# A block of fp32 matmuls ahead of the first projection of a fused attention layer

## The chip, the cores and the metric

The kernel runs on the 8 cores of one Trainium2 chip, as two dies of four cores. Each core does the same program on its own two sequences; the cores don't talk to each other. The metric is the device time of one execution in microseconds (us), that of the slowest core. Within 0.2% two kernels can't be told apart here.

## The reference, cut to what matters

x is [16, 2048, 1024] in fp32; every weight is 1024 x 1024.

```python
xn = layernorm(x)                                  # no gain, no bias
q, k, v = xn @ Wq.T, xn @ Wk.T, xn @ Wv.T          # 16 heads of 64
a = sliding_window_attention(q, k, v, 128)         # causal, chunks of 128 see their own and the previous chunk
s = a @ Wo.T
lhs_scale = max|xn| / 127 (by row);  rhs_scale = max|rhs| / 127 (by column)
q_lhs, q_rhs = round(xn / lhs_scale), round(rhs / rhs_scale)
g = silu((q_lhs @ q_rhs) * lhs_scale * rhs_scale)
y = x + s * g
```

## The kernel before, in words

A core's 4096 rows are worked in 32 chunks of 128 rows. The program is five instruction streams, one for each engine, each written out in full: an engine runs its stream in order, and waits on semaphores where it needs another's result. For each chunk TensorE (PE) makes five products of 128 x 1024 by 1024 x 1024 in bf16, each as 16 matmuls of 512 columns: `PROJ` for q, v, k and ffn into the PSUM tile `p_proj`, and the output product into `p_av`. Between them stand two groups of 16 score matmuls of 128 columns (`SCORES`, into `p_sc`) and 32 of 65 columns for attention times v (`AVS`, into `p_sc` again). ScalarE (ACT) empties `p_proj`, takes the exponentials and quantizes the rows; VectorE (DVE) does the layer norm (`LN1`, `LN2`), the mask, the division by the row sums, the ffn scaling and the result. The queue of SyncE (SP) issues the loads of x, the transposing DMAs and the stores. In the loop of a stream, step i does the main part of chunk i beside the projections of chunk i + 1 and the layer norm of chunk i + 2 or i + 3.

Ahead of the loop there is a prologue. GpSimd (POOL) issues the loads of the four attention weights, SP and ACT issue those of `rhs` in eight blocks, and DVE quantizes each block as it lands (lines 309 to 319). PE first works after the eighth block: one transpose of the eight column scales (line 495), which DVE copies to `rsrow8` (line 323), and then eight matmuls in fp32 (line 508) that spread the scales over all partitions in `p_proj`. DVE copies that out to `scr` (line 325), does `LN2(0)`, whose last instruction (line 294) writes the normalized chunk 0, and then `LN1(1)`. SP transposes `q_rhs` (line 161), loads chunks 1 and 2 of x (line 166) and transposes the quantized and the normalized chunk 0 (lines 210 and 214). PE's loop begins with `PROJ(0, "q", ...)`, whose matmuls all have line 519 and which waits for the transpose of chunk 0, for the q weights and for DVE's copy out of `p_proj`:

```python
                    Wv(tensor, f"trxn{c % 2}", 16 * (c // 2 + 1))
                    if c == 0:
                        Wv(tensor, "lwq", 128)
                    ...
                        W(tensor, "v", ("rsbe", 0))
                        PROJ(c, "q", bfp, XNT[c % 2], wbf, 0 * 8192)
```

`ident` is the 128 x 128 identity in fp32. `scr[:, XS[0]:...]` holds chunk 0 of x in fp32, loaded on the semaphore `lx0`. `IMM` issues a list of matmuls back to back and raises the semaphore `t` with the last of them. `Wv` waits for a semaphore's value, `W` for a named event.

Of the kernel before, what the change touches and what calls it, by code (L numbers as in the profile page):

```python
# [20 lines left out]
XS = [0, 1024, 2048, 3072]  # L21
# [52 lines left out]
def build(nchunk=NCHUNK):  # L74
# [15 lines left out]
    with ExitStack() as es:  # L90
# [3 lines left out]
        scr = sb("scr", [128, SCR_COLS], F32)  # L94
# [7 lines left out]
        ident = sb("ident_s", [128, 128], F32)  # L102
# [4 lines left out]
        p_sc = es.enter_context(nc.psum_tensor("p_sc", [128, 2048], F32))  # L107
# [21 lines left out]
        def Wv(eng, sname, value):  # L129
            if CUR[0].emit:  # L130
                eng.wait_ge(SEMS[sname], value)
# [361 lines left out]
        def emit_tensor(tensor):  # L493
# [5 lines left out]
            def IMM(mms, sname, tag):  # L499
                if CUR[0].emit:  # L500
                    last = None
                    for f in mms:
                        r = f()
                        last = r if r is not None else last
                    last.then_inc(SEMS[sname], 1)
                CUR[0].inc(sname, 1, (tag[0], tag[1]))
# [2 lines left out]
                                            sel[:, t * 128:(t + 1) * 128], rsrow8[:],  # L509
                                            start=True, stop=True)) for t in range(8)],  # L510
                "t", ("rsb", 0))

            def PROJ(c, name, lhs_t, lhs_base, rhs_t, rhs_base, half1_wait=None):
                mms = []
                for kc in range(8):
                    for half in range(2):
                        if kc == 0 and half == 1 and half1_wait is not None:
                            mms.append(half1_wait)
                        mms.append(lambda kc=kc, half=half: tensor.matmul(  # L519
                            p_proj[:, half * 512:(half + 1) * 512],  # L520
                            lhs_t[:, lhs_base + kc * 128:lhs_base + kc * 128 + 128],
                            rhs_t[:, rhs_base + kc * 1024 + half * 512:
                                  rhs_base + kc * 1024 + half * 512 + 512],
                            start=(kc == 0), stop=(kc == 7)))
                IMM(mms, "t", (name, c))
# [37 lines left out]
            for i in range(-2, nchunk + 2):  # L563
# [42 lines left out]
                if 0 <= i < nchunk:  # L606
# [7 lines left out]
                    for kc in range(8):  # L614
# [3 lines left out]
                        for half in range(2):  # L618
# [5 lines left out]
                                start=(kc == 0), stop=(kc == 7)))  # L624
# [25 lines left out]
        emit_vector(fe)  # L650
        emit_scalar(fe)
        emit_tensor(fe)
        emit_gpsimd(fe)

# [17 lines left out]
        @block.tensor  # L672
        def _(tensor):
            emit_tensor(tensor)
# [46 lines left out]
```

How the kernel before makes its waits and increments, by code:

```python
        def W(eng, sname, tag):  # L125
            if CUR[0].emit:
                eng.wait_ge(SEMS[sname], CUR[0].tag[(sname, tag)])
# [1 line left out]
        def Wv(eng, sname, value):  # L129
            if CUR[0].emit:
                eng.wait_ge(SEMS[sname], value)
# [1 line left out]
        def I(instr, sname=None, tag=None, n=1):  # L133
            if CUR[0].emit:
                bi = instr()
                if sname is not None:
                    bi.then_inc(SEMS[sname], n)
            if sname is not None:
                CUR[0].inc(sname, n, tag)
# [2 lines left out]
        def emit_sync(sync):  # L142
# [73 lines left out]
                      f"trxn{c % 2}", ("trxn", c), 16)  # L216
                if 0 <= i < nchunk:
                    c = i
                    b, cc = divmod(c, 16)
                    W(sync, "v", ("comb", c))
                    I(lambda b=b, cc=cc, c=c: sync.dma_start(
                        y_h[b, cc * 128:(cc + 1) * 128, :],
                        scr[:, OUTS[c % 2]:OUTS[c % 2] + 1024]),
                      "st", ("store", c), 16)
            if CUR[0].emit:
                sync.wait_ge(SEMS["st"], 16 * nchunk)
# [2 lines left out]
            def SW(instr):  # L229
                I(instr, "v", None)
                if CUR[0].emit:
                    vector.wait_ge(SEMS["v"], CUR[0].count["v"])
# [170 lines left out]
            def SWS(instr, sname=None, tag=None):  # L403
                I(instr, sname or "a", tag)
                if CUR[0].emit:
                    scalar.wait_ge(SEMS[sname or "a"], CUR[0].count[sname or "a"])
```

## Time and profile before

| | |
|---|---|
| median of 9 runs | 849.19 us (847.94 to 850.1) |
| the profiled execution, its own time | 848.81 us |
| span of its slowest core, from the first to the last instruction | 847.2 us |
| spans of the 8 cores | 841.5 to 847.2 us |
| PE busy | 665.2 us, 79% of the span |
| DVE busy | 530.0 us, 63% |
| ACT busy | 420.2 us, 50% |

The profiled execution's own time is 1.6 us more than the span of its slowest core: what lies around the first and the last instruction. The views below show core 4, unless another is named. An idle time is written beside the work that ended it, with the event that released that work.

### The profile page before, as it was taken

Reading aid. Unit: us, or ns where it says so; the run is one execution under the profiler, and the core shown is the slowest. Engines: PE = TensorE matmul, PEld = TensorE weight load, DVE = VectorE, ACT = ScalarE, POOL = GpSimd, SP = SyncE. Lnnn points to the kernel's source line nnn. Section 1 sums busy time; section 2 is a strip of 40 time slices with the busy share of each in tenths; the row PEclk is TensorE's granted clock in tenths of the full one; section 3 lists DMA queues with packets and bytes.
Section 4 is the critical chain, followed back from the end, with each engine's and each line's share of the span. In section 5 each row is a group of like instructions: output and inputs, shape, how many; then the busy total and the mean of one; then the engine's idle time right before and its main releaser. Section 6 shows DMA issues by size and latency. Waiting matters only on the chain.

```text
span 847.2 us, 13584 instructions; the slowest of 8 cores (841.5 to 847.2 us)
## 1 busy us (share of the span) xinstructions
PE 665.2 (79%) x4561; PEld 344.9 (41%) x4625; DVE 530.0 (63%) x1083; ACT 420.2 (50%) x481; POOL 17.2 (2%) x36
## 2 busy tenths in 40 slices
PE   0001588898889898888889888899888889988884
PEld 0001244444444444444444444444444444444442
DVE  3644257666666667766766666666776666666633
ACT  0001355556555566655555655556665555565541
POOL 8000000000000000000000000000000000000000
PEclk9999999999999999999999999999999999999995
DMA  7999245554444454444554434554335555444431
GB/s 162 197 208 189 61 82 107 112 107 105 89 89 111 113 112 97 101 103 106 106 113 112 99 86 91 113 113 113 94 97 110 106 107 112 113 100 89 63 63 62
DMA packets 194066, 91.29 MB, mean 108 GB/s; under 512 B 180296, under 2 KB 180680, under 8 KB 194000
## 3 DMA queue, kind: packets, MB, share of 16 engines
q1 hardware_dynamic: 188816, 79.95, 43.6%
q0 software_dynamic: 4608, 8.39, 6.2%
q10 hardware_dynamic: 576, 2.10, 0.8%
q8 instruction: 38, 0.62, 0.3%
q14 instruction: 28, 0.23, 0.1%
HBM read 37.98 MB, written 16.78 MB: 65 GB/s over the span
## 4 chain that ended last, share of the span: by engine, by line
PE 41%; DVE 30%; issue 14%; DMA 8%; ACT 3%; SPq 2%; DVEq 1%; ACTq 0%
PE p_proj L519 26%; PE p_av L619 12%; DVE sm L257 4%; DVE sm L247 4%; DVE scr L395 4%; DVE scr L384 4%; DVE bfp L341 3%; DMA scr<-rhst 3%; DVE scr L253 3%; DMA bfp<-bfp 3%; DVE scr L375 2%; DMA scr<-x 2%; SPq L161 1%; PE p_sc L555 1%; PE p_sc L558 1%
## 5 line engine op out<-in xcount | busy, mean ns | idle before, releaser
L519 PE MATMUL p_proj<-wbf,bfp 128*128 128x512 bf16 x1473 | 336.8, 381 | 61.0 <-DVE scr L375 22.9
L519 PEld LDWEIGHTS p_proj<-wbf,bfp 128*128 128x128 bf16 x1536 | 144.4, 98 | 224.0 <-issue 71.0
L619 PE MATMUL p_av<-wbf,bfp 128*128 128x512 bf16 x511 | 117.7, 384 | 4.2 <-DMA bfp<-bfp 3.1
L489 ACT ACTIVATE scr<-scr 128x1024 f32<-128x1024 f32 x32 | 33.8, 1057 | 174.5 <-DVE scr L375 174.5
L519 PE MATMUL p_proj<-qrhs,bfp 128*128 128x512 bf16 x512 | 115.7, 379 | 1.1 <-ACT bfp L474 1.1
L371 DVE SCALAR_TENSOR_TENSOR scr<-p_proj,sm,scr 128x512 f32<-128x512 f32 x32 | 24.0, 751 | 124.0 <-PE p_proj L519 123.9
L619 PEld LDWEIGHTS p_av<-wbf,bfp 128*128 128x128 bf16 x512 | 49.7, 99 | 67.9 <-issue 12.2
L519 PEld LDWEIGHTS p_proj<-qrhs,bfp 128*128 128x128 bf16 x512 | 50.0, 98 | 61.8 <-issue 1.5
L341 DVE TENSOR_TENSOR bfp<-bfp,mstd_s 128x2048 bf16<-128x2048 bf16 x60 | 71.0, 1222 | 4.7 <-ACT bfp L437 4.7
L459 ACT ACTIVATE q32t<-scr,sm 128x1024 int32<-128x1024 f32 x32 | 37.2, 1161 | 67.0 <-DVE bfp L319 67.0
L555 PE MATMUL p_sc<-bfp 128*128 128x65 bf16 x512 | 40.0, 195 | 36.4 <-DVE bfp L341 19.7
L536 PE MATMUL p_sc<-bfp 128*128 128x128 bf16 x512 | 64.8, 220 | 3.8 <-ACT bfp L421 3.8
L541 PE MATMUL p_sc<-bfp 128*128 128x128 bf16 x512 | 64.8, 220 | 0.0
L421 ACT ACTIVATE bfp<-p_sc 128x2048 bf16<-128x2048 f32 x32 | 59.5, 1859 | 0.0
L427 ACT CAST bfp<-p_proj 128x1024 bf16<-128x1024 f32 x32 | 32.4, 1012 | 49.5 <-PE p_proj L519 49.5
L555 PEld LDWEIGHTS p_sc<-bfp 128*128 128x128 bf16 x512 | 34.2, 98 | 53.2 <-issue 53.0
L536 PEld LDWEIGHTS p_sc<-bfp 128*128 128x128 bf16 x512 | 50.4, 99 | 11.6 <-issue 4.2
L495 PE MATMUL p_av<-ident_s,sm 128*8 128x128 f32 x1 | 0.4, 371 | 69.4 <-DVE bfp L319 69.4
L541 PEld LDWEIGHTS p_sc<-bfp 128*128 128x128 bf16 x512 | 50.4, 99 | 7.3
L443 ACT CAST bfp<-p_proj 128x512 bf16<-128x512 f32 x32 | 18.8, 589 | 65.1 <-PE p_proj L519 65.1
L247 DVE TENSOR_REDUCE sm<-scr 128x1 f32<-128x1024 f32 x32 | 38.8, 1211 | 15.8 <-DMA scr<-x 15.8
L384 DVE TENSOR_TENSOR scr<-p_av,scr 128x1024 f32<-128x1024 f32 x32 | 38.9, 1214 | 7.4 <-PE p_av L619 7.4
(63 smaller groups left out, 736.6 us busy)
## 6 DMA issues: line engine op xcount, KB each, us to landing
scr<-x SPq DMA_DIRECT2D x32, 512.0 KB, 4.6
y<-scr SPq DMA_DIRECT2D x32, 512.0 KB, 2.9
bfp<-bfp SPq DMA_TRANSPOSE x192, 3.2
scr<-rhst ACTq DMA_DIRECT2D x4, 512.0 KB, 8.1
wbf<-wqt POOLq DMA_DIRECT2D x8, 256.0 KB, 16.1
scr<-rhst SPq DMA_DIRECT2D x4, 512.0 KB
wbf<-wkt POOLq DMA_DIRECT2D x8, 256.0 KB, 25.5
wbf<-wvt POOLq DMA_DIRECT2D x8, 256.0 KB, 38.8
```

Source lines behind the costliest of these rows:

```text
L247: SW(lambda c=c: vector.reduce_sum(sm[:, SUMC:SUMC + 1], scr[:, XS[c % 4]:XS[c % 4] + 1024], AX.X))
L257: SW(lambda c=c, am=am: vector.reduce_max(sm[:, am:am + 1], scr[:, CEN[c % 2]:CEN[c % 2] + 1024], AX.X, apply_absolute_value=True))
L341: I(lambda e=ebv, r=erv, m=mkv: vector.tensor_tensor(e, r, m, ALU.mult), "v", ("e0m" if g == 0 else "e1m", c))
L384: SW(lambda c=c: vector.tensor_tensor(scr[:, T1_:T1_ + 1024], p_av[:, 0:1024], scr[:, GS[c % 2]:GS[c % 2] + 1024], ALU.mult))
L395: I(lambda c=c: vector.scalar_tensor_tensor(scr[:, GS[c % 2]:GS[c % 2] + 1024], scr[:, GS[c % 2]:GS[c % 2] + 1024], 1.0, scr[:, GPRE:GPRE ...
L421: I(lambda: scalar.activation(bfp2[:, ERAW:ERAW + 2048], p_sc[:, 0:2048], AF.Exp, scale=0.125), "a", ("e0", c))
L459: SWS(lambda c=c: scalar.activation(q32[:], scr[:, CEN[c % 2]:CEN[c % 2] + 1024], AF.Copy, scale=sm[:, QRA[c % 2]:QRA[c % 2] + 1], bias=MA ...
L519: mms.append(lambda kc=kc, half=half: tensor.matmul(p_proj[:, half * 512:(half + 1) * 512], lhs_t[:, lhs_base + kc * 128:lhs_base + kc * 1 ...
L536: mms.append(lambda hh=hh, qcol=qcol, tcol=tcol: tensor.matmul(p_sc[:, hh * 256:hh * 256 + 128], bfp[:, ktp + tcol:ktp + tcol + 128], bfp[ ...
L541: mms.append(lambda hh=hh, qcol=qcol, tcol=tcol: tensor.matmul(p_sc[:, hh * 256 + 128:hh * 256 + 256], bfp[:, ktc + tcol:ktc + tcol + 128] ...
L555: mms.append(lambda h=h, e0=e0: tensor.matmul(p_sc[:, h * 128:h * 128 + 65], bfp2[:, e0:e0 + 128], bfp[:, vp_ + h * 65:vp_ + h * 65 + 65], ...
L619: mms.append(lambda kc=kc, half=half, c=c: tensor.matmul(p_av[:, half * 512:(half + 1) * 512], bfp2[:, AOT[c % 2] + kc * 128:AOT[c % 2] + ...
```

## The change

One block of PE's prologue is new, between the eight matmuls that spread the scales and the loop. PE waits until chunk 0 of x is in SBUF, and then multiplies 512 columns of it by the identity, in fp32, 48 times, into the four banks of `p_sc` in turn. Nothing reads these results, and no other engine's stream is changed; the event `("warm", 0)` is waited for by nobody. The first scores of chunk 0 overwrite `p_sc`.

```diff
                                             sel[:, t * 128:(t + 1) * 128], rsrow8[:],
                                             start=True, stop=True)) for t in range(8)],
                 "t", ("rsb", 0))
+            Wv(tensor, "lx0", 16)
+            IMM([(lambda r=r: tensor.matmul(p_sc[:, (r % 4) * 512:(r % 4) * 512 + 512],
+                                            ident[:], scr[:, XS[0]:XS[0] + 512],
+                                            start=True, stop=True))
+                 for r in range(48)], "t", ("warm", 0))
 
             def PROJ(c, name, lhs_t, lhs_base, rhs_t, rhs_base, half1_wait=None):
```

## Rows read from the trace of the kernel before

**Rows 1.** The page, busy time by engine, and the slices of PE.
```profile
PE 665.2 (79%) x4561; PEld 344.9 (41%) x4625; DVE 530.0 (63%) x1083; ACT 420.2 (50%) x481; POOL 17.2 (2%) x36
...
PE   0001588898889898888889888899888889988884
```
**Rows 2.** PE's waits: who it waited for, us in total, times, longest.
```profile
PE p_av L495 <- DVE bfp L319: 69.4, 1, 69.4
PE p_proj L519 <- DVE scr L375: 22.9, 27, 0.8
...
PE p_proj L519 <- DVE sm L260: 15.4, 1, 15.4
```
**Rows 3.** Timeline, core 4: start, us, engine, line, operation, count, idle time before.
```profile
70.27 3.75 PE L508 MATMUL p_proj<-rsrow,sel_s 8*128 8x128 f32 x16 [0.53 <-DVE rsrow L323]
...
78.94 0.75 DVE L294 TENSOR_SCALAR bfp<-scr,sm 128x1024 bf16<-128x1024 f32 x1
...
83.67 3.41 SPq L214 DMA_TRANSPOSE bfp<-bfp  x1
...
89.46 5.22 PE L519 MATMUL p_proj<-wbf,bfp 128*128 128x512 bf16 x16 [15.44 <-DVE sm L260]
...
94.77 1.01 ACT L427 CAST bfp<-p_proj 128x1024 bf16<-128x1024 f32 x1 [21.91 <-PE p_proj L519]
...
96.03 3.61 PE L519 MATMUL p_proj<-wbf,bfp 128*128 128x512 bf16 x16 [1.36 <-ACT bfp L427]
```
**Rows 4.** Line 508, core 4: durations min/median/max, first and last start.
```profile
L508 PEld LDWEIGHTS p_proj<-rsrow,sel_s x16: 284/328/328, 70.2 to 73.4; 8*128 8x128 f32 x16
L508 PE MATMUL p_proj<-rsrow,sel_s x16: 416/416/549, 70.3 to 73.6; 8*128 8x128 f32 x16
```
**Rows 5.** Timeline, core 4: two weight loads among the first projection's matmuls.
```profile
90.27 0.15 PEld L519 LDWEIGHTS p_proj<-wbf,bfp 128*128 128x128 bf16 x1 [0.28 <-issue]
90.70 0.15 PEld L519 LDWEIGHTS p_proj<-wbf,bfp 128*128 128x128 bf16 x1 [0.28 <-issue]
```
**Rows 6.** The same two PE pieces on cores 7, 1 and 6, in that order.
```profile
70.71 3.75 PE L508 MATMUL p_proj<-rsrow,sel_s 8*128 8x128 f32 x16 [0.53 <-DVE rsrow L323]
89.41 5.51 PE L519 MATMUL p_proj<-wbf,bfp 128*128 128x512 bf16 x16 [14.96 <-DMA bfp<-bfp]
...
65.01 3.75 PE L508 MATMUL p_proj<-rsrow,sel_s 8*128 8x128 f32 x16 [0.53 <-DVE rsrow L323]
85.35 4.91 PE L519 MATMUL p_proj<-wbf,bfp 128*128 128x512 bf16 x16 [16.59 <-DVE sm L257]
...
85.97 6.19 PE L519 MATMUL p_proj<-wbf,bfp 128*128 128x512 bf16 x16 [17.09 <-DVE sm L257]
```
**Rows 7.** Spans and granted clock of the cores.
```profile
core 1: 842.6 us, clock 0.988
...
core 4: 847.2 us, clock 0.988
...
core 7: 847.1 us, clock 0.988
```
**Rows 8.** Timeline: q of chunk 1, its first pieces, core 4; then core 6.
```profile
113.44 4.55 PE L519 MATMUL p_proj<-wbf,bfp 128*128 128x512 bf16 x13 [0.16 <-issue]
...
110.07 3.69 PE L519 MATMUL p_proj<-wbf,bfp 128*128 128x512 bf16 x16 [2.62 <-DMA bfp<-bfp]
```
**Rows 9.** Stretches of core 4: busy (count) by engine, granted clock, DMA share, GB/s.
```profile
85.00:90.00 5.00, 0.54 (x2) 0.28 (x3) 3.66 (x6) 0.00 (x0) 0.00 (x0) 1.00 0.80 194
110.00:120.00 10.00, 6.88 (x35) 3.31 (x37) 6.57 (x9) 4.74 (x5) 0.00 (x0) 0.83 0.33 81
...
200.00:300.00 100.00, 89.34 (x616) 46.38 (x623) 66.55 (x134) 55.24 (x62) 0.00 (x0) 1.00 0.46 101
700.00:800.00 100.00, 90.28 (x612) 46.37 (x618) 64.73 (x143) 55.66 (x66) 0.00 (x0) 1.00 0.48 100
```
**Rows 10.** The chain that ended last, two of its pieces: start, us, what.
```profile
268.80 3.47 PE p_proj L519 x16
291.63 3.47 PE p_proj L519 x16
```

## The prediction

> **What bounds the kernel now.** The page's busy times come first: PE is busy 665.2 us of the span, far ahead of DVE, and its digits by slice are 8 and 9 from the sixth slice on and 0 in the first three [rows 1]. So there are two stages: a prologue of some 90 us in which PE does next to nothing, and a loop that PE sets. The chain that ended last shows the loop's pace: a projection of 16 matmuls starts at 268.80 and the corresponding one at 291.63, a step of 22.8 us, and PE's pieces lie on it in every step [rows 10]. PE's waits are the second view. In the loop the largest is 22.9 us in 27 parts of at most 0.8 us, so nothing large is idle there; the two single large waits are 69.4 us before PE's first instruction and 15.4 us before its first projection [rows 2]. The timeline, third, shows what fills the 15.4 us: PE ends the eight fp32 matmuls of line 508 at 74.02 (70.27 + 3.75), DVE writes the normalized chunk 0 at 78.94, SP issues its transpose at 83.67, and the projection begins at 89.46 [rows 3]. The waits name DVE line 260 as releaser; that is only the last event beside it, and core 7 names the DMA [rows 6], which is the one PE's wait asks for. From there on PE is on the path, since ACT's copy of q at 94.77 had waited 21.91 us for it, and v follows that copy at 96.03 [rows 3].
>
> **The change part by part.** Three things count: how long 48 matmuls take, when they may start, and what the first projection gains by following them.
>
> *Start.* The added wait is for chunk 0 of x, which DVE read long before; it costs nothing. PE's order puts the block behind line 508, whose last record starts at 73.6 [rows 4], so the block starts at about 73.8. It waits for no other engine, and what is queued behind it on PE is the whole loop, the first projection at its head. Its results go to `p_sc`, which nobody else touches before the first scores, and DVE's copy of line 325 is released by the eighth matmul of line 508, ahead of the block. The other streams are unchanged up to their waits for PE.
>
> *Length.* An fp32 matmul of this shape is not in the trace; the two nearest rows give its cost. Line 508 is 8 matmuls written in the program and 16 records in the trace, spaced 3.3/15 = 0.22 us [rows 4] (0.213 by its 3.75 us less one record's latency: (3.75 - 0.55)/15). So one fp32 matmul is two records and 0.427 us for 128 columns. In bf16 at the same low clock 512 columns take 0.43 us, the distance of two weight loads of the first projection [rows 5], or 0.107 us for 128. Hence fp32 costs four times bf16 by column. At full speed the 16 bf16 matmuls of v take 3.61 us, of which about 0.38 is the last one's latency: 0.2155 us each [rows 3]. One added matmul is 4 x 0.2155 = 0.862 us, and 48 are 41.4 us. The weight loads of line 508 take 0.33 us against a spacing of 0.21 [rows 4], so they overlap the matmuls even there; a record of 512 columns gives them 0.43 us even at full speed, and I cost them at nothing. Bounds: at the bf16 price for all of it, 48 x 0.2155 = 10.3 us; at the low clock throughout, 48 x 1.707 = 81.9 us; with every one of 96 loads exposed at half of 0.33, 15.7 us more.
>
> The Trainium skill (FP8 and Floating Point Precision, TensorE Precision Notes) says that true fp32 makes four passes through the array. The two rows give the same factor, and the rival below turns on whether it holds for a block of 128 rows and 512 columns.
>
> *Clock.* PE's two levels are seen in the spacing: 0.43 us for 512 columns is 1.2 GHz and 0.2155 is 2.4 GHz. The granted clock reads 1.00 in 85 to 90 us [rows 9], although the first matmuls there run at half speed, so in the prologue I go by the spacing. The first projection takes 5.22 us where a full-speed one takes 3.61 [rows 3], and 5.51, 4.91 and 6.19 us on cores 7, 1 and 6 [rows 6]: 1.3 to 2.6 us lost by a slow beginning. The added block will meet this slow beginning itself. Line 508 has kept PE busy for 3.75 us at the low level, which may count in full (0 to 0.7 us lost) or not at all (1.3 to 2.6 us). I take 1.0 us.
>
> *Sum, core 4.* 73.8 + 41.4 + 1.0 = 116.2: there the first projection starts, in place of 89.46, so 26.7 us late. Everything that it waits for is done by then: before, it was there by 89.46. It then runs at full speed, 3.61 us in place of 5.22, 1.6 us back. Net 25.1 us. On core 7, which starts line 508 0.44 us later, it is 27.2 - 1.9 = 25.3 us [rows 6]. What is behind the projection moves by as much: ACT's copy is released by PE, v by that copy, and the later transposes on SP's queue and DVE's `LN2(1)` hang on ACT's stream, which takes its work in order. DVE had `LN1(1)` done when the projection started, so it has nothing to be early with. Nor is there slack in the loop to take up the delay: idle pieces of 0.8 us that come from PE, ACT and DVE handing work round do not shrink when all three begin late. The cores bear this out already. Core 1 starts its first projection 4.11 us before core 4 (85.35 against 89.46) and ends 4.6 us before it (842.6 against 847.2) [rows 6, 7]: what is lost in the prologue is lost at the end.
>
> Both cores come to 872.3 us of span. The profiled execution's own time is 848.81, 1.6 above its span, so 873.9; its median over nine runs is 0.4 higher, so **874.3 us**, 25.1 more than 849.19.
>
> One later piece may move by itself. The first projection of chunk 1 has 13 matmuls in 4.55 us on core 4, where core 6 has 16 in 3.69 [rows 8], and the granted clock is 0.83 in 110 to 120 us [rows 9]: the clock falls after a sparse stretch and costs up to 1.8 us there. The sparse stretch stays as it is, 25 us later, so the dip may come, or not, as on core 6. I leave it at nothing, with -1.8 in the range.
>
> **The rivals.**
> *The block fits into the gap, and the kernel is no slower.* For this the array must take a full fp32 block at the bf16 rate. Then 48 x 0.2155 = 10.3 us, and with 2.6 us of slow beginning it ends at 86.7, inside the gap that ends at 89.46; the first projection gains up to 1.6 us: 847.6. The point from which it decides is (89.46 - 73.8)/48 = 0.326 us for one matmul. Against it: line 508 costs 0.427 us for a quarter of the columns. For it only that this line's eight rows are another shape. 4%, half on each side of the 0.2% bound (1.7 us).
> *PE stays at 1.2 GHz through the block,* because work with mostly zero weights does not raise the clock: 81.9 us, the first projection at 155.7, 66.2 us late and with nothing gained: 915.4. For it: all of line 508 ran at that level for 3.75 us. Against it: bf16 matmuls rose after 2.6 to 5.2 us of work (twice the loss), and line 508 was shorter than the longer of these. 5%.
> *Eight cores that stream without any pause get a reduced clock.* The nearest row is 0.83 [rows 9]: 41.4/0.83 = 49.9 us, 8.5 more, 882.8. Against it: in the loop, which all eight cores run at once, core 4's PE is 89 or 90 us busy of 100 and its granted clock is 1.00 [rows 9]. 5%.
> The Trainium skill (TensorE: Matmul & The Clock Gate, Seeing it yourself) states for this a limiter that takes a die to 13/16 of the clock once three of its cores run dense matmuls, depending on the data. By its figure the block would be 41.4 x 16/13 = 51.0 us, 9.6 more, an estimate from that page. This case's loop speaks against it at granted 1.00.
> *The weight loads show:* 15.7 us more, 890. Line 508 overlapped them at a quarter of the columns; 3%.
>
> **How the numbers follow.** The forecast has 83%. Its own range: the slow beginning from 0 to 2.6 us (-1.0 to +1.6), the later dip gone (-1.8), 0.001 us in a matmul's spacing (0.2), and the spread of the runs (1 us either way): 870.3 to 877.1. I give 869 to 880, with one microsecond or two for a step that I have put wrongly; it leaves out the four rivals, 17%. Slower by over 0.2% (the least that a measurement tells from no change): 96%; within 0.2%: 2%; faster: 2%.
>
> **What would show it.** On the added line: 96 PE records from about 73.8 to 116, spaced 0.43 us after a beginning at 0.85; the first projection at 116 in 3.6 us, with no idle time before it; ACT's copy of q at about 121 in place of 94.77; the loop's step still 22.8 us. A spacing of 0.85 throughout, one of 0.11, one of 0.52, or a gap between the block and the first projection would each show a rival. If the first projection is late by 26.7 us and the span grows by much less, the step that fails is that the delay is carried whole to the end.

## The result, and the profile after

The changed kernel takes 874.05 us (median of 9 runs), against 849.4 us for the kernel before (28 runs). The ratio is 1.0292, with a 95% interval of 1.0283 to 1.0301. That is 24.7 us more, where 25.1 were forecast. One of the nine executions took 928 us, with the cores of one die at a granted clock of 0.88 to 0.91; ratios and intervals leave such executions out, the medians given here and below do not.

The page of the kernel after (busy time and count of the engines, then PE in the 40 slices):

```profile
span 873.1 us, 13776 instructions; the slowest of 8 cores (865.2 to 873.1 us)
...
PE 707.9 (81%) x4656; PEld 363.7 (42%) x4721; DVE 530.8 (61%) x1083; ACT 420.1 (48%) x481; POOL 17.2 (2%) x36
...
PE   0008988888999889888988888888888988898884
```

PE is busy 42.7 us more than in [rows 1], while DVE and ACT are where they were. PE's slices 4 and 5, which read 1 and 5 before, now read 8 and 9. The span grew by less than the added work, 25.9 us, since part of it fell into time that was idle.

The timeline of core 2 after, on which the same pieces as in [rows 3] stand (start, us, engine, line, operation, count):

```profile
69.02 3.75 PE L508 MATMUL p_proj<-rsrow,sel_s 8*128 8x128 f32 x16 [0.53 <-DVE rsrow L323]
72.69 44.12 PE L513 MATMUL p_sc<-scr,ident_s 128*128 128x512 f32 x96
116.87 3.40 PE L524 MATMUL p_proj<-wbf,bfp 128*128 128x512 bf16 x15
121.63 3.61 PE L524 MATMUL p_proj<-wbf,bfp 128*128 128x512 bf16 x16 [1.36 <-ACT bfp L427]
...
120.36 1.01 ACT L427 CAST bfp<-p_proj 128x1024 bf16<-128x1024 f32 x1 [48.76 <-PE p_proj L524]
```

Line 513 is the added block (96 records for 48 matmuls) and follows line 508 without a gap. The first projection (line 524 here, 519 before) has no idle time before it. One of its 16 records is missing from the trace, so it starts one spacing earlier than printed, at 116.65. Its 15 records in 3.40 us are the full-speed pace that v shows with 16 in 3.61. ACT's copy of q came at 120.36; it had waited 48.76 us for PE, against 21.91 before [rows 3].

The weight loads of the block on that core give its pace, since each record has one load (start, us, count):

```profile
76.27 0.34 PEld L513 LDWEIGHTS p_sc<-scr,ident_s 128*128 128x128 f32 x1 [0.52 <-issue]
77.12 0.34 PEld L513 LDWEIGHTS p_sc<-scr,ident_s 128*128 128x128 f32 x1 [0.52 <-issue]
77.98 0.24 PEld L513 LDWEIGHTS p_sc<-scr,ident_s 128*128 128x128 f32 x1 [0.52 <-issue]
78.46 0.19 PEld L513 LDWEIGHTS p_sc<-scr,ident_s 128*128 128x128 f32 x1 [0.24 <-issue]
78.89 0.19 PEld L513 LDWEIGHTS p_sc<-scr,ident_s 128*128 128x128 f32 x1 [0.24 <-issue]
...
115.80 0.19 PEld L513 LDWEIGHTS p_sc<-scr,ident_s 128*128 128x128 f32 x1 [0.24 <-issue]
```

Up to 77.98 the loads are 0.85 us apart, from 78.46 on 0.43. The load at 78.46 is the 9th and the one at 115.80 the last of 96: (115.80 - 78.46)/87 = 0.429 us a record, 0.858 a matmul. Between a load's end and the next one's start lie 0.24 us, so the loads set nothing.

The chain that ended last, by line, now holds the block (shares of the span):

```profile
PE p_proj L524 27%; PE p_av L624 12%; PE p_sc L513 5%; DVE sm L257 4%; DVE scr L395 4%; DVE scr L384 4%; DVE sm L247 4%; DVE bfp L341 3%; DMA scr<-rhst 3%; DVE scr L375 2%; DVE scr L253 2%; DMA bfp<-bfp 2%; DMA scr<-x 2%; PE p_sc L560 1%; PE p_sc L563 1%
```

The new name is `p_sc` at line 513 with 5% of 873 us, 44 us: the whole block lies on the path. PE's waits in the loop are 23.2 us for line 375, as in [rows 2], and its wait of 15.4 us before the first projection is gone.

Seen over all cores, the profiled executions split in two numbers: when the first projection starts, and how long it is from there to the end.

| kernel | first projection starts, mean of 8 cores | from there to the end, mean |
|---|---|---|
| before | 87.4 | 757.3 |
| after | 114.9 | 755.1 |

The start is 27.5 us later and the rest 2.2 us shorter: 2.0 by the first projection, 5.6 us before and 3.6 after in the mean, and 0.3 by chunk 1's q projection, 5.2 us before and 4.9 after. What follows that projection takes 728.7 us before and 728.8 after.

### The profile page after: what moved, and what is told of

Read it like the earlier page. It is cut to its first block, busy times and chain, and to the rows that moved or that the text cites. A ratio compares the mean times of both kernels' runs of the same rounds, so it can differ in the third digit from the quotient of the medians.

```text
span 873.1 us, 13776 instructions; the slowest of 8 cores (865.2 to 873.1 us)
## 1 busy us (share of the span) xinstructions
PE 707.9 (81%) x4656; PEld 363.7 (42%) x4721; DVE 530.8 (61%) x1083; ACT 420.1 (48%) x481; POOL 17.2 (2%) x36
## 4 chain that ended last, share of the span: by engine, by line
PE 46%; DVE 28%; issue 13%; DMA 7%; ACT 3%; SPq 1%; DVEq 1%; ACTq 0%
PE p_proj L524 27%; PE p_av L624 12%; PE p_sc L513 5%; DVE sm L257 4%; DVE scr L395 4%; DVE scr L384 4%; DVE sm L247 4%; DVE bfp L341 3%; DMA scr<-rhst 3%; DVE scr L375 2%; DVE scr L253 2%; DMA bfp<-bfp 2%; DMA scr<-x 2%; PE p_sc L560 1%; PE p_sc L563 1%
## 5 line engine op out<-in xcount | busy, mean ns | idle before, releaser
L524 PE MATMUL p_proj<-wbf,bfp 128*128 128x512 bf16 x1473 | 335.5, 380 | 45.3 <-DVE scr L375 23.2
L270 DVE TENSOR_SCALAR sm<-sm 128x1 f32<-128x1 f32 x32 | 4.9, 154 | 74.9 <-ACT scr L467 74.9
L443 ACT CAST bfp<-p_proj 128x512 bf16<-128x512 f32 x32 | 18.8, 588 | 65.1 <-PE p_proj L524 65.1
```

The source lines that it names most:

```text
L524: mms.append(lambda kc=kc, half=half: tensor.matmul(p_proj[:, half * 512:(half + 1) * 512], lhs_t[:, lhs_base + kc * 128:lhs_base + kc * 1 ...
```

## The experiments

Two theories stood against each other from the start. Theory A is the prediction's: the block streams at the fp32 price, what lies beyond the idle time is carried whole to the end, and the projection's slow beginning is given back. The rivals put the cost elsewhere: in a fixed price of the block or in its number of instructions, in a reduced clock, or in an effect on the other engines; or they had the loop take up a part.

**n96: twice the count.**

```diff
-                 for r in range(48)], "t", ("warm", 0))
+                 for r in range(96)], "t", ("warm", 0))
```

> 96 of the fp32 matmuls in place of 48. Theory A (the block streams at 0.43 us a record once the clock is up, and all that lies beyond the idle 15.6 us is carried whole to the end): 48 more matmuls at 0.859 us are 41.2 us more than the changed kernel's 874.1, so 915.3 us. Rival B (part of the 25 us is a fixed cost of having the block, or the loop takes up part of a delay): the second 48 cost clearly less than 41 us, 905 or below. Rival C (a longer unbroken stream on eight cores is granted less clock): records of 0.52 us somewhere in the block, and more than 920 us.

Measured: 914.8 us, ratio 1.0769 (1.0755 to 1.0783). The second 48 matmuls cost 40.7 us, 0.85 each; A had forecast 915.3 us. The stretches of core 0 show what rival C asked for (busy and count by engine, granted clock, DMA share, GB/s):

```profile
80.00:110.00 30.00, 30.00 (x71) 13.30 (x70) 3.66 (x6) 0.00 (x0) 0.00 (x0) 1.00 0.27 61
110.00:150.00 40.00, 40.00 (x94) 17.67 (x93) 0.00 (x0) 0.00 (x0) 0.00 (x0) 1.00 0.00 0
```

93 loads in 40 us are 0.43 us a record, at the end of 80 us of streaming as in its first half, and on the eight cores the 192 records took 84.1 to 85.7 us. Rivals B and C fall. That the granted clock also reads 1.00 alone would not do, as the section on the hardware shows; the spacing does.

**n24: half the count.**

```diff
-                 for r in range(48)], "t", ("warm", 0))
+                 for r in range(24)], "t", ("warm", 0))
```

> 24 of the fp32 matmuls: the first count that is well beyond the idle time. Theory A: 24 x 0.859 = 20.6 us and 2.2 us for the slow beginning are 22.8, 7.2 beyond the idle 15.6 us; less the 1.6 us that the projection gains, 5.6 us more than before: 854.9 us. Rival B (something takes up a small delay, such as the later waits for DMAs, and only the rest shows): 849 to 852 us.

Measured: 855.04 us, ratio 1.0064 (1.0048 to 1.008), beside 849.52 for before: 5.5 us more, where A said 5.6. In the profile the first projection starts 6.8 us later than before in the mean of the cores, and from there to the end it is 755.3 us, as in the changed kernel: nothing takes up a delay of 7 us.

**bf48: the same count in bf16.**

```diff
-            Wv(tensor, "lx0", 16)
+            Wv(tensor, "lwq", 128)
...
-                                            ident[:], scr[:, XS[0]:XS[0] + 512],
+                                            mstd[:, 0:128], wbf[:, 0:512],
```

> 48 matmuls of the same shape in bf16 instead of fp32 (the mask as weights, 512 columns of the q weights as moving data, behind a wait for the q weights, 48 times). Theory A: a bf16 matmul costs a quarter, 0.2155 us; 10.3 us and 1.5 to 2.8 us for the slow beginning end 2.5 to 4 us inside the idle time. The time is then 849.2 us if the clock falls again in those 3 us, 847.5 us if not; in no case above 850. Rival B (it is the number of matmuls, or the place, that costs, not the four passes): near 874.

Measured: 848.83 us, ratio 0.9993 (0.9979 to 1.0007). With the same number of matmuls of the same shape in the same place the whole cost is gone, so it is the four-fold time of fp32. The three cores 1, 0 and 5 of this run, in that order, block and first projection:

```profile
73.68 12.31 PE L513 MATMUL p_sc<-wbf,mstd_s 128*128 128x512 bf16 x48
89.11 3.61 PE L524 MATMUL p_proj<-wbf,bfp 128*128 128x512 bf16 x16 [3.12 <-DVE sm L257]
...
85.15 5.30 PE L524 MATMUL p_proj<-wbf,bfp 128*128 128x512 bf16 x16 [2.25 <-DVE sm L257]
...
90.56 5.37 PE L524 MATMUL p_proj<-wbf,bfp 128*128 128x512 bf16 x16 [5.57 <-DMA bfp<-bfp]
```

Three cores of eight kept the higher clock into the projection, after 2.4 to 3.2 us without work; five lost it, after 2.3 to 5.6 us. One lost it after a shorter pause than one that kept it, so the pause's length alone does not tell. No gain can be measured.

**early48: the same block, in PE's idle time ahead of the scales.**

```diff
+            Wv(tensor, "lx0", 16)
+            Wv(tensor, "ldw", 96)
+            IMM([(lambda r=r: tensor.matmul(p_sc[:, (r % 4) * 512:(r % 4) * 512 + 512],
+                                            ident[:], scr[:, XS[0]:XS[0] + 512],
+                                            start=True, stop=True))
+                 for r in range(48)], "t", ("warm", 0))
             W(tensor, "v", ("cast", 7))
             I(lambda: tensor.transpose(p_av[0:8, 0:128], sm[:, RSTL:RSTL + 8], ident[:]),
```

> The same 48 fp32 matmuls, but at the head of PE's stream, behind waits for chunk 0 of x and for the first block of rhs, ahead of the transpose of the scales. Theory A: the block starts at 18 to 20 us and takes 44 us, so it ends at 62 to 64, before the transpose at 64 to 69 us; it lies in idle time, costs nothing and, as PE idles after it, gives nothing: 849.2 us, within 1 us. On a core whose first block of rhs lands late it may end up to 3 us after the transpose could have started, and cost that. Rival C (the block's power or its port traffic slows the loads, DVE or the later clock): clearly more than 850 us, with DVE's instructions of line 309 to 319 longer or later.

Measured: 849.39 us, ratio 0.9994 (0.9985 to 1.0003). Core 0 of it, the block, the transpose and the first projection:

```profile
20.91 44.02 PE L505 MATMUL p_sc<-scr,ident_s 128*128 128x512 f32 x96 [20.91 <-DMA scr<-rhst]
69.73 0.37 PE L510 MATMUL p_av<-ident_s,sm 128*8 128x128 f32 x1 [4.80 <-DVE bfp L319]
...
90.59 5.28 PE L525 MATMUL p_proj<-wbf,bfp 128*128 128x512 bf16 x15 [16.21 <-DVE sm L257]
```

The same 44 us of work cost nothing where PE has nothing to do. The transpose is still released by DVE's line 319, and DVE is not slowed: line 309 takes 1.22 us an instruction here and before. Line 508 begins at 68.6 us in the mean of the cores, against 67.5 before and 68.2 and 68.3 in bf48 and n96, which leave the stretch ahead of the scales as it was; so a slowing of the loads by some tenths of a microsecond is not excluded, but none shows in the time. Ending over 25 us before the projection, the block gives it nothing either: on all eight cores it took 5.1 us or more.

**n14: a count that fits into the idle time.** The same edit with `range(14)`.

> 14 of the fp32 matmuls. Theory A: 14 x 0.859 = 12.0 us and 1.5 to 2.8 us for the slow beginning, so the block ends 0.8 to 2 us inside the idle time; the first projection starts when it did before, and at full speed, in 3.6 us in place of 4.9 to 6.2: 1.3 to 2.6 us less than before, 847.5 us. Rival B (a block costs something even when it fits, or the clock has fallen again when the projection starts): 849.2 us or more, with the projection at 5 us or more. Rival D (what the projection gains is lost at the next wait for a DMA): projection in 3.6 us and 849.2 us.

Measured: 847.85 us, ratio 0.998 (0.9969 to 0.999): the 1.7 us that were expected, and no more than the 0.2% from which two kernels can be told apart. Of the eight cores seven have the first projection in 3.6 us. Core 0, and core 1, the one that lost the clock:

```profile
73.80 14.13 PE L513 MATMUL p_sc<-scr,ident_s 128*128 128x512 f32 x28
88.70 3.61 PE L524 MATMUL p_proj<-wbf,bfp 128*128 128x512 bf16 x15 [0.77 <-DVE sm L257]
...
85.95 5.30 PE L524 MATMUL p_proj<-wbf,bfp 128*128 128x512 bf16 x16 [2.31 <-DVE sm L260]
```

**rows8: the same count and columns, with 8 rows.** The prediction had taken 1.0 us for the block's own slow beginning, and the trace after showed 1.5 to 3.0. The question was whether the eight fp32 matmuls of line 508 had failed to count because they use 8 of 128 rows.

```diff
-                                            ident[:], scr[:, XS[0]:XS[0] + 512],
+                                            sel[:, 0:128], sel[:, 0:512],
```

> The 48 fp32 matmuls of 512 columns with 8 rows in place of 128 (the selector matrix by itself). Theory F (the eight fp32 matmuls ahead of the block did not count towards the higher clock because only 8 of 128 rows worked): records spaced 0.85 us throughout, 82 us, the first projection near 155 and slow at its beginning, 915 us. Rival G (they did not count because they were few or came too early, not for their rows): the clock rises in this block as in the changed kernel, 42 to 44 us, 874 us.

Measured: 916.17 us, ratio 1.0776 (1.0755 to 1.0796), theory F. The weight loads and matmuls of the block, with durations min/median/max, and what follows it:

```profile
L513 PEld LDWEIGHTS p_sc<-sel_s x96: 328/332/332, 72.5 to 153.0; 8*128 8x128 f32 x96
L513 PE MATMUL p_sc<-sel_s x96: 1055/1056/1057, 72.8 to 153.8; 8*128 8x512 f32 x96
...
154.81 5.99 PE L524 MATMUL p_proj<-wbf,bfp 128*128 128x512 bf16 x16
```

(153.8 - 72.8)/95 = 0.853 us a record from the first to the last, 1.2 GHz for 82 us of work without a pause, and the projection behind it begins slowly as if PE had idled. So the count, the columns and fp32 by themselves do not raise the clock. What is left is the eight rows or the data: here the weights and the moving data are both mostly zeros. The changed kernel's block, whose weights are mostly zeros too but which has 128 rows and x as moving data, did raise it.

**c128: 128 columns in place of 512.**

```diff
-            IMM([(lambda r=r: tensor.matmul(p_sc[:, (r % 4) * 512:(r % 4) * 512 + 512],
-                                            ident[:], scr[:, XS[0]:XS[0] + 512],
+            IMM([(lambda r=r: tensor.matmul(p_sc[:, (r % 4) * 512:(r % 4) * 512 + 128],
+                                            ident[:], scr[:, XS[0]:XS[0] + 128],
```

> The 48 fp32 matmuls with 128 columns each in place of 512. Theory A (time goes by columns, four passes for each): records spaced 0.11 us at full speed, 48 x 0.2155 = 10.3 us and the slow beginning of 1.5 to 2.8 us; all fits into the idle time, 847.5 to 849.5 us. Rival E (the weight loads of fp32, 0.19 us each and two for a matmul, bound it at few columns): spacing near 0.19 us at full speed, 18.2 us and the slow beginning, 20.5 us; 3 us more than before, 852. It also shows whether 128 rows with few columns raise the clock, where the eight rows with 128 columns of the scale spreading did not.

Measured: 850.32 us, ratio 1.0003 (0.9992 to 1.0015); by the ratio it is at the upper end of A's range, and E's 852 us lies above the interval. The block takes 12.4 to 13.8 us on the cores, as A said (10.3 and the slow beginning), so a load of 0.19 us does not hold back records spaced 0.11 (on core 0, 36 of them begin from 80 to 84 us). But it leaves 3.5 to 5.3 us of idle time, and on all eight cores the projection took 5.1 us or more: no gain. These 96 short records with 128 rows did raise the clock: the block is shorter than the 20 us it would take at 1.2 GHz.

**n14fill: a second filling, in front of chunk 1's q projection.** This kernel and the next four look for one that is faster than the kernel before. The projection of [rows 8] takes 5.3 or 5.4 us on most cores, before and after, behind a wait of 2.6 us.

```diff
                     c = i + 1
+                    if i == 0:
+                        IMM([(lambda r=r: tensor.matmul(
+                            p_av[:, (r % 2) * 512:(r % 2) * 512 + 512],
+                            mstd[:, 0:128], wbf[:, 0:512], start=True, stop=True))
+                            for r in range(11)], "t", ("fill", 0))
                     Wv(tensor, f"trxn{c % 2}", 16 * (c // 2 + 1))
```

> 14 fp32 matmuls in the prologue as in n14, and 11 bf16 matmuls of 512 columns into p_av (idle there) between the first scores of chunk 0 and the q projection of chunk 1, where PE waits 2.6 us for a transposing DMA. Theory A (the second dip of the clock comes from that sparse stretch and costs 1.7 us): 11 x 0.2155 = 2.4 us fit into the wait, the projection of chunk 1 takes 3.6 us in place of 5.3 on all cores, 1.7 us less than n14's 847.9: 846.2 us. Rival (the clock falls there whatever is in the wait, or the matmuls outlast it): projection of chunk 1 at 5.3 us or started later, and 848 to 849 us.

Measured: 847.01 us, ratio 0.9975 (0.9965 to 0.9985). Core 0, the filling and what it protects:

```profile
108.35 2.54 PE L578 MATMUL p_av<-wbf,mstd_s 128*128 128x512 bf16 x11
111.13 3.61 PE L524 MATMUL p_proj<-wbf,bfp 128*128 128x512 bf16 x16 [0.25 <-DMA bfp<-bfp]
```

The slow beginning of chunk 1's projection is gone on all eight cores, but the time is only 0.8 us under n14's, in another session, and 1.7 were expected. (A session is a group of runs on one chip, with the kernel before timed beside them; n14 and n14fill ran on different chips.) In this profile two cores lost the clock before the first projection, against one in n14's.

**n14b, fillonly and n16fill: the parts beside each other in one session.** n14b is n14's kernel again; fillonly has only the second filling; n16fill has both, with `range(16)`.

> n14 once more, beside the next two on one chip, since n14 and n14fill were timed in different sessions. Theory A: 847.8 us, ratio 0.998.

> The 11 bf16 matmuls in the wait before the q projection of chunk 1 alone, without a block in the prologue. Theory A (each slow beginning of a projection is a cost of its own, carried to the end): first projection 5 us or more as before, chunk 1's at 3.6 us in place of 5.3: 847.8 us, ratio 0.998. Rival (n14fill's gain is n14's alone, and the second dip's loss is taken up later or moves on): 849.5 us.

> n14fill with 16 in place of 14 fp32 matmuls: 13.7 us and 2.2 us of slow beginning reach to within 0.3 us of the end of the idle time, on some cores beyond it. Theory A: the first projection is fast on all cores (in n14fill two of eight fell back after 2.4 and 3.2 us of idle time), and where the block outlasts the idle time the projection is up to 1 us late: 846 to 847 us, ratio 0.996 to 0.997. Rival: the lateness costs more than the cores kept fast gain, 847.5 to 849 us.

Measured, beside 851.8 us for before, which took 849.5 in the sessions above: n14b 851.7, ratio 1.0001 (0.9992 to 1.001); fillonly 852.1, ratio 0.9996 (0.9982 to 1.001); n16fill 848.64, ratio 0.9965 (0.9952 to 0.9977). n14's gain is not there. Core 5 of n14b and core 5 of n16fill, block and first projection:

```profile
73.26 13.83 PE L513 MATMUL p_sc<-scr,ident_s 128*128 128x512 f32 x28
91.16 6.43 PE L524 MATMUL p_proj<-wbf,bfp 128*128 128x512 bf16 x16 [4.07 <-DVE sm L257]
```
```profile
73.96 16.20 PE L513 MATMUL p_sc<-scr,ident_s 128*128 128x512 f32 x32
90.23 3.61 PE L524 MATMUL p_proj<-wbf,bfp 128*128 128x512 bf16 x16
```

The idle time was longer here: fillonly, which leaves it empty, shows 16.2 to 19.35 us on its cores, where the kernel before showed 15.0 to 17.1 at first [rows 6]. Fourteen matmuls left 4.07 us on core 5, and the projection began slowly on four cores, among them the three slowest, which set the time; that fits the missing gain, though no run varied the idle time alone. Sixteen left nothing on core 5 and at most 2.2 us on the others, and the projection took 3.6 us on all eight. fillonly's projection of chunk 1 took 3.61 us on all cores, and still nothing could be measured: expectation A failed there, its 0.998 lying just below the interval. n16fill's ratio of 0.9965 is what A had expected of it.

**n16: n16fill without the second filling.** The change with `range(16)`.

> 16 fp32 matmuls in the prologue and nothing else: n16fill without its second part, since fillonly gained nothing that could be measured (ratio 0.9996) although its projection of chunk 1 ran in 3.6 us on all cores. Theory A (both slow beginnings are carried to the end): ratio 0.998, 1.2 to 1.7 us more than n16fill's 0.9965. Rival (the gain of n16fill is that of its prologue block alone): 0.9965 here too. The first projection in 3.6 us on all or nearly all cores in both.

Measured: 851.02 us, ratio 0.999, in a session of its own with before at 851.47. Its interval (0.9976 to 1.0004) hardly touches n16fill's (0.9952 to 0.9977), with before within 0.4 us in the two sessions. That speaks for a share of the second filling, but n16's profile has the first projection slow on its slowest core (4.97 us) and chunk 1's at 5.3 on several, so the two shares can't be told apart.

The traces show where the rest of the 1.7 us went. Means of the eight cores, in us, from the first projection's start to the end:

| kernel | first projection | from its end to chunk 1's q | chunk 1's q | after it | sum |
|---|---|---|---|---|---|
| before | 5.6 | 17.9 | 5.2 | 728.7 | 757.3 |
| n14 | 3.8 | 18.0 | 4.9 | 728.1 | 754.8 |
| n14fill | 4.0 | 17.9 | 3.6 | 728.3 | 753.8 |
| fillonly | 5.7 | 18.8 | 3.6 | 728.4 | 756.4 |

From n14 to n14fill the second filling gained 1.2 us and not 1.7, because two of n14's cores had their chunk 1 projection in 3.6 us already; 0.2 went back to the first projection, slow on one core more. From before to fillonly it gained 1.6 us, but chunk 1's projection started 0.9 us later after the first: the transposing DMA that it waits for landed later, on all eight cores. n14fill has the same filling without this delay, so whether the filling or that chip caused it stays open.

## Why the prediction was right

By its steps:

- *Start.* The block begins with line 508's last record, at 72.69 on core 2 and 3.7 us behind that line's start on every core. By that it would have been 73.95 on core 4 of before, where 73.8 was taken. Right, within 0.15 us.
- *Length, 41.4 us.* 96 x 0.429 = 41.2 us. The factor of four between fp32 and bf16, from the 0.427 us of an 8-row matmul, held for 128 rows and 512 columns. The rule of the Trainium skill (FP8 and Floating Point Precision, TensorE Precision Notes), four passes, agrees with this measurement. The loads were hidden, as costed.
- *Slow beginning, 1.0 us.* Too small. From the block's start to the projection's start it is 42.7 to 44.2 us on the cores; less 41.2, that is 1.5 to 3.0 us, 2.3 in the mean. The prediction had left open whether line 508 would count in full or not at all; rows8 shows that matmuls with eight rows did not raise the clock in 82 us, so the larger value, 1.3 to 2.6 us, was the one to take.
- *What the projection gains.* 1.6 us were taken for core 4; over the cores it went from 5.6 us to 3.6, 2.0.
- *Everything behind moves by as much.* The first projection starts 27.5 us later in the mean of the cores and the spans grow by 25.3. n24 and n96 add the straight line: 5.5, 24.7 and 65.3 us more for 24, 48 and 96 matmuls. The slope is 0.80 from the first to the second and 0.85 from the second to the third.
- *The sum* came out at 874.3 where 874.05 was measured, and so much agreement was luck. Against the mean of the cores, five errors nearly cancel: the slow beginning was 1.3 us too small and the start 0.15 too early; against that, the idle time that the block fills is 16.1 us in the mean, where core 4, on which the sum was made, had 15.4 (0.7 too much delay), the projection gained 0.4 more, and chunk 1's q projection 0.3. The spans grew by 25.3 us in the mean of the cores and 25.9 for the slowest, the medians by 24.7. The range of 869 to 880 is what the rows carried.
- *The rivals.* The block did not fit into the gap. The decision point of 0.326 us for one matmul is borne out from both sides, if coarsely: bf48 (0.2155) costs nothing and the change (0.858) costs 25 us. The reduced clock did not come: n96 streams on all eight cores for 84 us or more at 0.43 us a record. The limiter that the Trainium skill states (TensorE: Matmul & The Clock Gate, Seeing it yourself) would have given 0.53 us, an estimate from its 13/16. The Trainium skill makes it depend on the data, and the block's weights are an identity, so this streaming alone would not refute it. But the loop, with random x and weights on all eight cores, keeps 3.47 us for 16 matmuls as well [rows 10], so the limiter does not show in the executions profiled here. The rival of 1.2 GHz throughout, 915.4 us, did not come true for the change, but it is what rows8 measured, 916.2.
- *The later dip* of the clock, at chunk 1's q projection, was there on seven of eight cores before and on six after: leaving it at nothing was right within 0.3 us.

## What to carry to other kernels

Filler matmuls ahead of a critical product cost nothing up to the end of PE's idle time and their full time beyond it; count them as matmuls by columns, with fp32 at four times bf16, and not by how many they are. What they can give back is small and can be read ahead of time: the difference between the first product's duration and that of the same product in the loop, here 1.3 to 2.6 us of 849. They give it only if they end shortly before the product's start: with 0 to 2.2 us between (n16fill) all eight cores kept the higher clock, with 3.5 to 5.3 us (c128) none did. Where DMAs set that start it moves from session to session, here by 1.1 us in the mean of the cores (an idle time of 16.1 us before, 17.3 in fillonly) and by more than 2 on single ones, so a fixed count that wins in one session (n14) may win nothing in the next (n14b). The best kernel here, n16fill, was 0.35% faster than before, in one session of five runs.

## What the runs showed of the hardware

Matmuls with 8 of 128 rows, from the selector matrix, ran at 1.2 GHz for 82 us without a pause (rows8), where 128 rows of fp32 reached 2.4 GHz after 3 to 6 us (twice the 1.5 to 3.0 lost). Whether it is the rows or the share of zeros was not separated.

In the traces read here the granted clock reads 1.00 from the start to the first time that it falls, whatever the array does. In rows8 (core 0, first line) 88 loads in 75 us are 0.85 us a record, 1.2 GHz, and it reads 1.00. The second line is core 4 of the kernel before, with line 508 in it; the others are core 0 of early48, where the clock had fallen once by 70 us:

```profile
75.00:150.00 75.00, 75.00 (x89) 29.22 (x88) 6.15 (x18) 0.00 (x0) 0.00 (x0) 1.00 0.16 35
...
70.00:90.00 20.00, 4.29 (x18) 3.77 (x19) 7.88 (x23) 2.67 (x4) 0.00 (x0) 1.00 0.98 191
...
25.00:40.00 15.00, 15.00 (x35) 6.54 (x34) 8.81 (x15) 0.00 (x0) 0.00 (x0) 1.00 1.08 208
60.00:70.00 10.00, 5.20 (x13) 1.98 (x11) 7.17 (x12) 0.32 (x1) 0.00 (x0) 0.85 1.09 205
70.00:90.00 20.00, 3.85 (x17) 3.48 (x16) 7.38 (x21) 3.03 (x4) 0.00 (x0) 0.50 0.91 192
```

The same eight matmuls of the scales in 3.75 us stand in 70 to 90 us here at 0.50 and in the kernel before at 1.00. A mean clock over the whole execution is therefore no measure of such a prologue; the spacing of equal matmuls is.

An fp32 weight load of 128 columns took 0.19 us at 2.4 GHz and 0.34 at 1.2, about twice a bf16 one's 0.098 and 0.15, and behind records of 128 columns spaced 0.11 us (c128) it still did not set the pace.
